# Expert layer 1 by seven block products (Strassen's recursion) instead of eight, and a new order of the products in a step

## The reference

```python
Wh = layernorm(x) @ W;  e = leaky_relu(Wh @ a1 + (Wh @ a2)^T) + log(adj + 1e-6)
x1 = x + softmax(e) @ Wh
```

```python
xn = layernorm(x1);  w = softmax(mean_over_graphs(xn) @ Wr + br)     # 128 nodes x 8 experts
h = relu(bn1(xn @ W1[e] + b1[e]));  h = relu(bn2(h @ W2[e] + b2[e]))
out = x1 + sum_e w[:, e] * (h @ Wo[e] + bo[e])
```

## Time and profile before

| | |
|---|---|
| median of three runs | 2537.67 us |
| profiled execution, span of its instructions | 2535.1 us |
| TensorE matmuls busy | 2453.0 us, 97% |
| VectorE, ScalarE, GpSimd busy | 58%, 63%, 16% |
| HBM traffic | 116 MB, mean 46 GB/s |
| graph stage | 0 to about 345 us |
| mixture | about 345 to 2535 us |

### The profile page before, as it was taken

One profiled execution on the slowest core, in us unless ns is written; L12 is line 12 of the kernel. 1 busy time (PEld: TensorE's weight loads), 2 busy tenths in 40 slices (PEclk: granted clock), 3 DMA queues, 4 the chain that ended last, 5 costly groups with the idle time before them and its releaser, 6 DMA issues.

```text
span 2535.1 us, 38086 instructions
## 1 busy us (share of the span) xinstructions
PE 2453.0 (97%) x14000; PEld 2125.7 (84%) x14000; DVE 1479.0 (58%) x2160; ACT 1592.8 (63%) x2142; POOL 408.1 (16%) x450
## 2 busy tenths in 40 slices
PE   7888789999999999999999999999999999999998
PEld 6666668888888888888888888888888888888887
DVE  6999965555555555555555555555555555555554
ACT  6777746666666666666666666666666666666665
POOL 5888820000000000000000000000000000000000
PEclk9999989999999999999999999999999999999999
DMA  6666510000000000000000000000000000000000
GB/s 190 214 203 202 188 61 26 26 12 13 25 25 25 25 25 25 25 25 25 25 25 25 25 2 22 25 25 25 25 25 25 25 25 25 25 25 25 14 11 25
DMA packets 88991, 116.02 MB, mean 46 GB/s; under 512 B 4572, under 2 KB 76680, under 8 KB 88968
## 3 DMA queue, kind: packets, MB, share of 16 engines
q1 hardware_dynamic: 88968, 115.73, 14.2%
HBM read 82.16 MB, written 33.55 MB: 46 GB/s over the span
## 4 chain that ended last, share of the span: by engine, by line
PE 86%; ACT 0%; DVE 0%; issue 0%
PE ps_wide L158 56%; PE ps_y L1096 28%; PE ps_t L145 1%; ACT h L923 0%; DVE h_lo L1003 0%; DVE h2w L998 0%; ACT h_hi L948 0%; DVE out_sb L1010 0%; ACT h_hi L935 0%; PE ps_t L1112 0%; ACT featT L958 0%; PE ps_t L1107 0%; DVE h_lo L991 0%
## 5 line engine op out<-in xcount | busy, mean ns | idle before, releaser
L923 ACT ACTIVATE h<-ps_wide,bn_cols 128x512 f32<-128x512 f32 x1024 | 791.0, 776 | 494.7 <-PE ps_wide L158 487.4
L991 DVE TENSOR_TENSOR h_lo<-h,h_hi 128x1024 fp32r<-128x1024 f32 x256 | 313.4, 1224 | 604.1 <-ACT h_hi L935 604.1
L1096 PE MATMUL ps_y<-w_hi,h_hi 128*128 128x256 f32 x2048 | 572.2, 279 | 2.2 <-DVE h_lo L1003 2.2
L1096 PE MATMUL ps_y<-w_lo,h_hi 128*128 128x256 f32 x2048 | 571.8, 279 | 0.0
L1096 PE MATMUL ps_y<-w_hi,h_lo 128*128 128x256 f32 x2048 | 570.8, 279 | 0.0
L1003 DVE TENSOR_TENSOR h_lo<-h2w,h_hi 128x1024 fp32r<-128x1024 f32 x256 | 376.5, 1471 | 290.7 <-ACT h_hi L948 290.7
L948 ACT ACTIVATE h_hi<-h2w 128x1024 fp32r<-128x1024 f32 x256 | 271.4, 1060 | 336.5 <-DVE h2w L998 336.5
L158 PE MATMUL ps_wide<-xT_hi,w_hi 128*128 128x512 f32 x1024 | 405.6, 396 | 3.3 <-ACT h L923 3.3
L158 PE MATMUL ps_wide<-h_hi,w_hi 128*128 128x512 f32 x1024 | 407.7, 398 | 0.0
L158 PE MATMUL ps_wide<-xT_lo,w_hi 128*128 128x512 f32 x1024 | 405.8, 396 | 0.0
L158 PE MATMUL ps_wide<-xT_hi,w_lo 128*128 128x512 f32 x1024 | 405.4, 396 | 0.0
(11 more groups left out here) (118 smaller groups left out, 2441.4 us busy)
## 6 DMA issues: line engine op xcount, KB each, us to landing
x_sb<-in_x SPq DMA_DIRECT2D x32, 512.0 KB, 3.5
res<-in_x SPq DMA_DIRECT2D x32, 512.0 KB, 4.5
x_scratch<-x SPq DMA_DIRECT2D x32, 512.0 KB, 3.0
x1t<-x_scratch SPq DMA_DIRECT2D x32, 512.0 KB, 4.5
resb<-x_scratch SPq DMA_DIRECT2D x32, 512.0 KB, 5.2
out<-out_sb SPq DMA_DIRECT2D x32, 512.0 KB, 3.6
adj_sb<-in_adj SPq DMA_DIRECT2D x32, 256.0 KB, 3.8
w_stage<-in_L_ffn_W SPq DMA_DIRECT2D x16, 256.0 KB, 3.8
```

The lines of the kernel that those rows point to most:

```text
L923: last = nc.scalar.activation(h[:, c, :], psum[:, c, :], ACT.Relu, bias=bn_cols[:, row + 1, C * e + c:C * e + c + 1], scale=bn_cols[:, row ...
L991: nc.vector.tensor_tensor(h1_lo[p][:, :, :], h1[:, :, :], h1_hi[p][:, :, :].bitcast(F32), ALU.subtract).then_inc(lo1_done, 1)
L1096: mm = nc.tensor.matmul(ps_y[:, b4, :], h[:, c, cols], w[:, i, c, :], start=(e == 0 and n == 0 and b4 % per_bank == 0), stop=(e == E - 1 a ...
```

## The change

**Layer 1.** The 2x2 blocks of W1 (input half x output half) and of the tile (input half x node half, H = 256 nodes) are multiplied with seven block products in place of eight. The block sums of the tile, T1 to T4, are made by GpSimd (`tile_sums`), those of the weights in the graph stage, also by GpSimd; all seven blocks of each are kept in high and low parts (`xq_hi`, `xq_lo`, `wq_hi`, `wq_lo`). Each block product is three products of 256 columns:

```diff
+                def strassen(out_ps, e, q, start, stop):
+                    terms = ((wq_hi, xq_hi), (wq_lo, xq_hi), (wq_hi, xq_lo))
+                    for n, (w, x) in enumerate(terms):
+                        mm = nc.tensor.matmul(out_ps, w[:, e, q, :], x[:, q, :], start=start and n == 0,
+                                              stop=stop and n == len(terms) - 1, skip_group_check=True)
```

```diff
-                    nc.scalar.activation(h1_hi[u[1] % 2][:, :, :], h1[:, :, :], ACT.Copy).then_inc(hi1_done, 1)
+                    act.wait_ge(z1_done, uno(u) + 1)
+                    act.wait_ge(z2_done, uno(u) + 1)
+                    wait(act, l2_done, C * uno(u))
+                    nc.scalar.activation(h1_hi[:, :, :], z[:, :, :], ACT.Relu).then_inc(hi1_done, 1)
+                def sum_1(u):
+                    dve.wait_ge(p3_done, uno(u) + 1)
+                    dve.wait_ge(v2_done, uno(u) + 1)
+                    nc.vector.scalar_tensor_tensor(out=z[:, 0, :], in0=ps_l1[:, 1, :], ...
```

**Order of a step.** TensorE's new queue (`new` is the unit of layer 1, `prev` the one before, `done` three before):

```diff
+                    if exists_unit(new):
+                        wait(pe, z2_done, uno(new))
+                        strassen(a_sum, e, 0, True, False).then_inc(p1_done, 1)
+                        wait(pe, z1_done, uno(new))
+                        strassen(x_p5, e, 1, True, False)
+                        strassen(x_p2, e, 2, False, False).then_inc(p2_done, 1)
+                    if exists_unit(prev):
+                        pe.wait_ge(lo1_done, uno(prev) + 1)
+                        wait(pe, r2_done, C * uno(prev))
+                        layer_2(prev, 0)
+                    if exists_unit(new):
+                        pe.wait_ge(v1_done, uno(new) + 1)
+                        strassen(a_sum, e, 3, False, False)
+                        strassen(a_p4, e, 4, False, False).then_inc(p4_done, 1)
+                    if exists_unit(prev):
+                        layer_2(prev, 1)
+                    if exists_unit(new):
+                        pe.wait_ge(v2_done, uno(new) + 1)
+                        strassen(a_sum, e, 5, False, True).then_inc(p7_done, 1)
+                    if exists_unit(done):
+                        pe.wait_ge(lo2_done, uno(done) + 1)
+                        layer_3(done, 0)
+                    if exists_unit(new):
+                        pe.wait_ge(z2_done, uno(new) + 1)
+                        strassen(x_p5, e, 6, False, True).then_inc(p3_done, 1)
+                    if exists_unit(done):
+                        layer_3(done, 1)
+                    if e == E - 3 and exists_unit(unit(t, n + 3)):
+                        tile_transpose(pe, unit(t, n + 3)[0], ps_t_x)
```

More of the change, by code:

```diff
@@ L133, in tile_normalise @@
[L133 to L139, removed]
+                last = nc.vector.tensor_scalar(x1t[:, b4, :], x1t[:, b4, :], mean_all[:, t, b4:b4 + 1],
+                                               rstd_all[:, t, b4:b4 + 1], ALU.subtract, ALU.mult)
@@ L147, in tile_transpose, with tile_copy @@
             last.then_inc(xT_ready, 1)
-        def tile_high(act, t, ps_x):
+        def tile_copy(act, t, ps_x):
             act.wait_ge(xT_ready, t + 1)
-            nc.scalar.activation(xT_hi[:, :, :], ps_x, ACT.Copy).then_inc(xhi_done, 1)
+            wait(act, xqlo_done, 3 * t)
+            for c, (first, step) in enumerate(((B11, B12 - B11), (B21, B22 - B21))):
+                last = nc.scalar.activation(xs[:, first:first + step + 1:step, :],
+                                            ps_x[:, c, :].rearrange("p (t n) -> p t n", n=H), ACT.Copy)
+            last.then_inc(xs_copied, 1)
@@ L534, in _ @@
                 over_groups(act, step)
+                for group in range(3):
+                    tile_high(act, 0, group)
             @block.vector
@@ L669, in _ @@
                 over_groups(dve, step)
+                for group in range(3):
+                    tile_low(dve, 0, group)
                 dve.wait_ge(x1_done, G)
@@ L708, in project, with step @@
                     return mm
-                def step(g):
+                def step(g, layer):
                     a = ago(g, 1)
@@ L1064, in _, with step @@
-                over_tiles(dve, first, body)
+                def step(t, n):
+                    new, prev, old = unit(t, n), unit(t, n - 1), unit(t, n - 2)
+                    done = unit(t, n - LEAD)
+                    if exists_unit(prev):
+                        low_1(prev)
+                    if starts(new, 1):
+                        feature_mean()
+                    if starts(new, 2):
+                        gate_softmax()
+                        dve.wait_ge(w_bc_done, 1)
+                    if exists_unit(old):
+                        gate_2(old)
+                        low_2(old)
+                    if new[1] == E - 1 and exists_unit(unit(t, n + 1)):
+                        tile_low(dve, unit(t, n + 1)[0], 0)
+                    if exists_unit(new):
+                        sum_2(new)
+                    if new[1] == E - 1 and exists_unit(unit(t, n + 1)):
+                        tile_low(dve, unit(t, n + 1)[0], 1)
+                    if exists_unit(new):
+                        sum_1(new)
+                    if new[1] == E - 1 and exists_unit(unit(t, n + 1)):
+                        tile_low(dve, unit(t, n + 1)[0], 2)
+                    if done[1] == E - 1 and exists_unit(done):
+                        out_add(done[0], 0)
+                        out_add(done[0], 1)
+                    if new[1] == E - 4 and exists_unit(unit(t, n + 4)):
+                        tile_normalise(dve, unit(t, n + 4)[0])
```

667 lines of the change are left out of this document (365 added, 302 removed).

## The result

The changed kernel takes 2882.8 us (median of four, 2881.4 to 2888.1) against 2537.8 us before: 1.136 times the time, interval 1.1346 to 1.1378. The forecast was 2846 us in a range of 2725 to 2935. The profiled execution took 2881.4 us, its span 2879.7.

The account below looks back on a forecast made before the run. TensorE bounds stage two before the change; then latency loops of 9.17 us a step. 350 + 3 + 36 + 2320 + 119 + 16 = 2844 us profiled, 2846 us as the runs' median, range 2725 to 2935.

Parts of the forecast that it names:

- the 0.35 us: Layer 1 on TensorE: 21 products of 256 columns for 12 of 512 save this per step, 90 us if TensorE stays the bound.
- The round trip: Each step, q6 through sum_1, high_1, low_1 to layer 2 has 2.45 us of cover; 0.35 saved becomes 0.77 us lost.
- Both loops: TensorE's loop from layer 2 to low_1, and one through the helpers: 9.17 and 9.15 us a step.
- The size of a plain step: Stage two, each step: 9.17 us against 8.40 before; 253 steps make 2320 us.
- the second loop: Low_1, gate_2, high_2, low_2, relu_2, v3, sum_2, q6, sum_1, high_1, low_1, without TensorE's long run: 9.15 us.
- Once a tile: Extras per tile on a loop with no slack (normalise, out_add, copies, GpSimd, sums): 3.85 us, 119 us over 31 tiles.
- GpSimd's addition to resb: After out_add, GpSimd's addition now meets low_1 on VectorE: +1.8 us a tile, ends 0 and 2.4.
- Start and end: Stage two starts at about 350 us; +3 for output weights and clock, 36 filling the pipeline, 16 for the end.
- TensorE as the bound: Rival for stage two: TensorE never waits and gets faster, 2468 us; chance 3%.
- the outer loop alone: Rival: sum_2 comes in time and GpSimd falls into gaps; 8.97 us a step, 1.3 a tile, 2717 us; chance 12%.
- more of GpSimd: Rival: both GpSimd stretches land fully on low_1 or gate_2, 7 us a tile, 2944 us; chance 10%.
- The falling clock: Rival: TensorE's waits in each step lower its clock in a tenth of the steps, 119 us more, 2965 us; chance 3%.

Follow-up runs that it names:

- e5_seven_only: The kernel before, only layer 1 changed to 21 products of 256 columns, without block sums (output not the reference's): 2459.3 us, ratio 0.9691.
- e7_extra: The changed kernel with block product q0 made twice, 0.35 us more TensorE work a step: 2884.3 us, ratio 1.1359.
- e2_own_h2w: The changed kernel with h2w in its own buffer, so relu_2 waits for gate_2 and not low_2: 2868.3 us, ratio 1.1298.
- e6_split: The changed kernel with high_1 and low_1 in halves, the half from sum_2 split while q6 runs: 2767.5 us, ratio 1.0896.
- e1_one_wait: The changed kernel with high_1 waiting for one semaphore in place of three: 2873.1 us, ratio 1.1312.
- e4_queues: e3_order with gate_2 ahead of low_1 on VectorE and q6 after two products of layer 2's second half: 2673.5 us, ratio 1.0530.
- e3_order: The changed kernel with layer 3 ahead and layer 2 at the step's end on TensorE, relu_2's first half behind v3: 3034.4 us, ratio 1.1955.
- e9_copies: e4_queues with the next tile's preparation moved earlier and spread, its two copies placed before and behind v2: 2515.7 us, ratio 0.9914.

## Why the prediction was right, and what its terms measured

**What bounds, and the 0.35 us.** Right: e5_seven_only shows the saving (80 of the 90 us), e7_extra that it is worthless in the changed order, since 90 us of work were put back for 1.5 us.

**The round trip.** Right in mechanism: TensorE waits for low_1 and for sum_2, at the forecast places, with 207.5 us in the table (forecast some 200). Both loops bind together, as forecast: e2_own_h2w takes one away and gains 14 us; e6_split shortens what they share and the step falls by 0.98 us.

**The size of a plain step** was the term that was too small: 9.53 instead of 9.17 us, 253 x 0.36 = 91 us. By pieces of the second loop (forecast, measured): low_2 to relu_2 1.25, 1.33; v3 0.67, 0.70; sum_2 0.57, 0.59; q6 0.73, 0.81; sum_1 0.65, 0.66; sum_1 to high_1 0.70, 0.87. The last is nearly half of it: sum_1 takes 0.751 us and not the 0.68 of the line through 256 and 1024 elements (it lay within its ends, 0.61 and 0.82), and high_1 starts 0.12 after its end, not 0.02. I had taken the shortest hop seen for all of them; e1_one_wait shows that 0.09 of this one hangs on the waits in front of the instruction. Most of the rest is of the same two kinds: sum_2, which stands in q6's 0.81, also takes 0.751, and relu_2 starts 0.10 us after low_2's end, not 0.02. Copies of v at 0.557 (forecast 0.55) and low_1 at 1.23 were right.

**Once a tile** was too large: 1.84 instead of 3.85, 31 x 2.0 = 62 us. The transposes cost nothing, as forecast, and so did normalise (forecast 0.2): low_1 starts 1.96 us after sum_1 with it and without. out_add cost 0.13 (0.3). The tile's sums and split made one step 1.40 longer (0.75 + 0.8 forecast, near enough). The error is GpSimd's addition to resb, forecast 1.8, measured as 0.2: GpSimd's and VectorE's timelines of the step after out_add,

```profile
1260.37 2.41 POOL L970 TENSOR_TENSOR resb<-resb,bias_out 128x1024 f32<-128x1024 f32 x1 [44.93 <-DMA resb<-x_scratch]
```

```profile
1260.50 0.75 DVE L1080 SCALAR_TENSOR_TENSOR z<-ps_wide,bn_cols,v 128x512 f32<-128x512 f32 x1 [0.72 <-PE ps_wide L1178]
1262.46 1.40 DVE L1087 SCALAR_TENSOR_TENSOR h_lo<-z,h_hi 128x1024 fp32r<-128x1024 f32 x1 [1.21 <-ACT h_hi L987]
```

show it 7.4 us after the output's store was issued (1253.02), not the 8.4 to 9.1 that the transfers' medians of before gave; now they land in 3.2 and 3.9 us. It ended at 1262.78, and low_1, due at 1262.46, met its last 0.32 us only: 1.40 us instead of 1.22. Over all 31 tiles low_1 is stretched by 0.20 us in the mean, from nothing in 13 tiles to 0.66. A forecast of a collision from two sums of some 9 us is no better than the error of each, which was 1 us here; in e6_split, where steps are a microsecond shorter, it does collide.

The Trainium skill (SBUF — State Buffer, Who interferes with whom) lets a VectorE instruction with at most one SBUF input, outside its 2-port modes, run freely beside GpSimd. This case's trace agrees: sum_1 at 1260.50, whose other input is in PSUM, took 0.75 us under GpSimd's addition, the same as without it, while low_1 and gate_2 with two SBUF inputs took 1.60 and 1.75 beside the tile's sums.

**Start and end.** The first product of stage two came at 353.2 us (forecast 350); layer 2 of step 3 at 392.03 (389). The two steps after it, which also bring Wo in, took 11.05 and 11.68 us from gate_2 to gate_2, 3.7 over two plain ones together. From 392.03 on, 253 x 9.53 + 31 x 1.84 + 3.7 + 16 make 2487.8, against 2487.7 to the end of the span. The 16 is the forecast's term and was not measured, so an agreement this close is chance.

Sum of the errors: 91 + 3 + 4 - 62 = +36 against the forecast's 2844, and the span measured 2879.7. The forecast was 1.3% low because errors of 91 and 62 us partly cancelled, not because each term was good to 1%.

**The rivals.** TensorE as the bound (2468 us) is refuted by the table of waits; the outer loop alone (2717) by q6's wait for sum_2, 96 us in the two rows; more of GpSimd (2944) by the rows above. The falling clock (2965) is refuted too: 1.00 from 1000 to 1500 us with two waits in each step. It was lower only in the first steps of stage two, for which the forecast had allowed. The frequent micro-idles of which the Trainium skill warns (TensorE: Matmul & The Clock Gate, A second HAM failure mode) did not make the clock swing here, though TensorE waited twice in each step, for 1.5 us at the longest. Single idle stretches of 2.4 us did so in e4_queues, in 17 tiles of 31.

## What to carry to other kernels

Work taken off the busiest engine is time won only while the order leaves that engine something to do: add up the round trip that a new dependency makes (last product, eviction, split, first product that needs it) and compare it with the work that stands between. Here each step became 1.13 us longer than before, which is 280 of the 345 us; with a whole layer's work between, and with the helpers' queues in an order to match, the same seven products win 23 us over the kernel before. The order of TensorE alone did not do it: e3_order has the cover, and is the slowest of all. When the plain step is short, the once-a-tile pieces decide: put each into a gap of its own engine, and never ahead of a copy for which TensorE waits.

## What the runs showed of the hardware that was not expected

- The hop from one engine's end to the next one's start isn't one number: sum_1 to high_1 took 0.12 us with three waits in front of high_1 and 0.03 with one; gate_2 to high_2, with its waits unchanged, took 0.03 us in one step and 0.11 in another.
- Idle stretches of one length are not always followed by the same clock: after 2.41 to 2.49 us without a product, TensorE went on at the level of 1.2 GHz in 17 tiles of e4_queues and at 2.4 GHz in 14; after 2.71 to 2.73 us in e3_order at 1.2 GHz in 16 of 30.
- A VectorE scalar_tensor_tensor of 512 elements with one input in PSUM takes 0.751 us; the line through the 256- and 1024-element rows of other operations gave 0.68.
- GpSimd and VectorE slow each other where VectorE has two SBUF inputs: a GpSimd sum of 128x256 took 0.74 us beside sum_2 in e9_copies, as it did alone, and 1.60 beside VectorE's low_1 and low_2 with two SBUF inputs in e4_queues, which took 1.67 and 1.75 there in place of 1.22.
